# A decayed-attention scan: the output product and the bias in fp32r passes, softplus in two pieces, results in place, and part of the values' work on GpSimd

## The reference

```
q = x @ W_q.T;  k = x @ W_k.T;  v = x @ W_v.T          # 64 positions, 8 heads of 64
b = (q * k).sum(-1) * SCALE                             # one number per head and position
a = -softplus(x @ W_alpha_w.T + W_alpha_b).sum(-1)      # one number per head and position
vs, vl = sign(v), log(|v| + EPS)
step: ln = logaddexp(a_t + ln, b_t)
      dec, new = a_t + nm, b_t + vl_t;  m = max(dec, new)
      ssum = sg * exp(dec - m) + vs_t * exp(new - m)
      sg = sign(ssum) (0 counts as +);  nm = m + log(|ssum| + EPS)
      y_t = (sg * exp(nm - ln)).sum over heads
out = y @ W_o.T
```

## Time and profile before

| | |
|---|---|
| median of 3 runs | 2053.11 us (2052.66 to 2054.73) |
| the profiled execution | 2054.83 us, span 2053.0 us |
| granted TensorE clock, mean | 0.941 of full |
| busy over the span | TensorE 1886.5, VectorE 1333.0, ScalarE 1125.2, GpSimd 136.0 us |
| decayed attention layer | about 1516 to 1831 us |

### The profile page before, as it was taken

One profiled execution on the slowest core, in us unless ns is written; L12 is line 12 of the kernel. 1 busy time (PEld: TensorE's weight loads), 2 busy tenths in 40 slices (PEclk: granted clock), 3 DMA queues, 4 the chain that ended last, 5 costly groups with the idle time before them and its releaser, 6 DMA issues. The chain is left out here.

```text
span 2053.0 us, 31444 instructions
## 1 busy us (share of the span) xinstructions
PE 1886.5 (92%) x10506; PEld 1503.4 (73%) x10506; DVE 1333.0 (65%) x2451; ACT 1125.2 (55%) x1864; POOL 136.0 (7%) x130
## 2 busy tenths in 40 slices
PE   7989985999997599999999999999968999889998
PEld 4657875999996578787878787878746767665664
DVE  4783547999995373636363636363538898877686
ACT  5762324888884353535454545454426676656663
POOL 0001000111110010000000000000000000002221
PEclk9999976999998799999999999999988988879999
DMA  6300042453524121101010101012031000020000
GB/s 234 107 31 1 2 167 82 162 195 125 193 72 174 62 83 42 36 31 39 27 50 17 51 15 51 15 51 81 17 119 63 1 1 1 1 88 0 1 21 21
DMA packets 22753, 129.81 MB, mean 63 GB/s; under 512 B 3602, under 2 KB 3858, under 8 KB 18963
## 3 DMA queue, kind: packets, MB, share of 16 engines
q1 hardware_dynamic: 17714, 112.59, 15.1%
q0 software_dynamic: 4960, 16.26, 2.4%
HBM read 116.51 MB, written 12.32 MB: 63 GB/s over the span
## 5 line engine op out<-in xcount | busy, mean ns | idle before, releaser
L116 PE MATMUL PS<-cT,qs 128*128 128x512 f32 x1152 | 300.3, 406 | 2.3 <-DVE qs L1682 2.2
L116 PE MATMUL PS<-pT,cN 128*128 128x512 f32 x1152 | 270.1, 392 | 1.7 <-DVE pT L1682 1.7
L116 PEld LDWEIGHTS PS<-cT,qs 128*128 128x128 f32 x1152 | 210.6, 189 | 52.3 <-issue 7.9
L116 PEld LDWEIGHTS PS<-pT,cN 128*128 128x128 f32 x1152 | 213.9, 188 | 45.4 <-DVE pT L1682 1.9
L116 PE MATMUL PS<-fw,xgT 128*128 128x384 f32 x1104 | 204.5, 340 | 5.7 <-DVE xgT L1224 5.7
L116 PEld LDWEIGHTS PS<-fw,xgT 128*128 128x128 f32 x1104 | 193.3, 190 | 9.2 <-DVE xgT L1224 6.3
L1677 DVE TENSOR_REDUCE nmax<-PS 128x1 f32<-128x512 f32 x128 | 87.6, 684 | 162.6 <-PE PS L116 162.5
L1224 DVE TENSOR_TENSOR fw<-W,fw 128x1536 fp32r<-128x1536 f32 x92 | 159.2, 1752 | 22.8 <-ACT fw L1147 22.8
L116 PE MATMUL PS<-xT,ws 128*128 128x512 f32 x576 | 155.1, 422 | 15.1 <-PEq L2575 8.7
L1582 ACT ACTIVATE qp<-PS 128x512 f32<-128x512 f32 x96 | 57.4, 598 | 189.6 <-PE PS L116 189.6
L1147 ACT ACTIVATE fw<-W 128x1536 fp32r x92 | 134.4, 1489 | 33.1 <-issue 33.1
(11 more groups left out here) (285 smaller groups left out, 3398.9 us busy)
## 6 DMA issues: line engine op xcount, KB each, us to landing
W<-in_fc SPq DMA_DIRECT2D x8, 3072.0 KB, 11.1
cT<-in_ctxT SPq DMA_DIRECT2D x16, 768.0 KB, 4.3
raw_pj<-in_proj SPq DMA_DIRECT2D x8, 1536.0 KB, 6.5
ct_in<-in_ctxT SPq DMA_DIRECT2D x16, 768.0 KB, 4.3
cn_in<-in_ctxN SPq DMA_DIRECT2D x16, 768.0 KB, 5.0
W<-in_w SPq DMA_DIRECT2D x2, 4096.0 KB, 13.7
routed_y<-y POOLq DMA_DIRECT2D x23, 256.0 KB, 2.3
W<-in_w SPq DMA_DIRECT2D x5, 1024.0 KB, 7.3
```

The source lines that it names most:

```text
L116: mm = nc.tensor.matmul(out, lhs(m, s), rhs(n, s), start=(opens and (s, m, n) == terms[0]), stop=((s, m, n) == terms[-1]))
```

## The change

- Work areas: `lg`, `q`, `vt`, `v0`, `s_`, `ep` lie in W0 where six others lay. `mag`, `soft`, `qk`, `veps`, `ear` and `sg` are gone: softplus works in `lg`, the products in `q`, the signed epsilon is written to `vt` itself, and `ear`, the maximum and the signed result share `ep`. `bv`, `ebv`, `bal`, `y_raw` lie in W0 too.
- The bias product of the A projection is two fp32r products (`one` x two parts of `bal`).
- The output product is a `split_product` with `yT` and `wo` in two parts. ScalarE makes the first parts (`first_y`, and `wo` once at chunk 0, j=5), GpSimd the rests (`rest_y`, and `wo` in one 128x2048 instruction).
- `take_a` keeps Abs and Exp at j=1; `take_log` follows `take_q` at j=2. VectorE's `softplus` moves from j=2 to j=3, before the maximum, and `products` from before to behind the maximum of j=3.
- `make_v` on VectorE keeps only the bit operation; GpSimd adds (`vt = v0 + vt`), and GpSimd takes `rest_v`.
- w16's load also waits for the rest of `wo`, because `wo` is now loaded where w16 goes.

```
-            nc.tensor.matmul(bank, ones[0:1, :], bal[0:1, :], start=True, stop=False)
+            for part in range(2):
+                nc.tensor.matmul(bank, one[0:1, :], bals[part][0:1, :], start=(part == 0), stop=False)
...
-                    pe.wait_ge(yT_sb, BASE + 2 + c + 1)
+                    pe.wait_ge(y_lo, BASE + c + 1)
...
-                    for k in range(DK):
-                        mm = nc.tensor.matmul(ps[3], yT[:, c % 2, k, :], wo[:, k, :], start=(k == 0), stop=(k == DK - 1))
-                    mm.then_inc(z_mm, 1)
+                    split_product(nc, ps[3], lambda part, k: yT[part][:, k, :],
+                                  lambda part, k: wo[part][:, k, :], DK).then_inc(z_mm, 1)
...
 GpSimd
+                def make_v(c):
+                    pool.wait_ge(veps_sb, BASE + c + 1)
+                    nc.gpsimd.tensor_tensor(vt, v0, vt, ALU.add).then_inc(vt_sb, 1)
+                def rest_v(c):
+                    pool.wait_ge(v_hi, BASE + c + 1)
+                    nc.gpsimd.tensor_tensor(vs[1][:, c % 2, :], vt, vs[0][:, c % 2, :].bitcast(F32),
+                                            ALU.subtract).then_inc(v_lo, 1)
+                def rest_y(c):
+                    pool.wait_ge(y_hi, BASE + c + 1)
+                    pool.wait_ge(z_mm, BASE + c)
+                    nc.gpsimd.tensor_tensor(yT[1][:, :, :].rearrange("p k t -> p (k t)"), y_raw,
+                                            yT[0][:, :, :].rearrange("p k t -> p (k t)").bitcast(F32),
+                                            ALU.subtract).then_inc(y_lo, 1)
+                ln.pool(pool, 0)
+                ln.pool(pool, 1)
+                make_v(0)
+                rest_v(0)
                 for c in range(NG):
-                    ln.pool(pool, c)
+                    if c + 2 < NG:
+                        ln.pool(pool, c + 2)
+                    if c + 1 < NG:
+                        make_v(c + 1)
+                        rest_v(c + 1)
+                    if c == 0:
+                        pool.wait_ge(wo_hi, BASE + 1)
+                        nc.gpsimd.tensor_tensor(wo[1][:, :, :], wo_in, wo[0][:, :, :].bitcast(F32),
+                                                ALU.subtract).then_inc(wo_lo, 1)
+                    else:
+                        rest_y(c - 1)
...
+                rest_y(NG - 1)
...
 ScalarE
-                    nc.scalar.activation(mag, mag, ACT.Exp, scale=-1.0).then_inc(ex_sb, 1)
+                    nc.scalar.activation(lg, lg, ACT.Exp, scale=-1.0).then_inc(ex_sb, 1)
+                def take_log(c):
                     act.wait_ge(ex_sb, BASE + c + 1)
-                    act.wait_ge(a_used, BASE + c)
-                    nc.scalar.activation(lg, mag, ACT.Ln, bias=cn[:, CN_ONE:CN_ONE + 1]).then_inc(lg_sb, 1)
+                    nc.scalar.activation(lg, lg, ACT.Ln, bias=cn[:, CN_ONE:CN_ONE + 1]).then_inc(lg_sb, 1)
...
+                def first_y(c):
+                    act.wait_ge(yT_sb, BASE + 2 + c + 1)
+                    act.wait_ge(z_mm, BASE + c)
+                    nc.scalar.activation(yT[0][:, :, :].rearrange("p k t -> p (k t)"), y_raw, ACT.Copy).then_inc(y_hi, 1)
...
                 first_w(0)
+                act.wait_ge(s_bal, BASE + 16)
+                nc.scalar.activation(one[:, :], ones[0:1, :], ACT.Copy)
+                nc.scalar.activation(bals[0][:, :], bal, ACT.Copy).then_inc(bal_hi, 1)
                 first_w(1)
...
                         elif j == 2 and c + 1 < NG:
                             take_q(c + 1)
-                        elif j == 3 and c + 1 < NG:
-                            first_v(c + 1)
+                            take_log(c + 1)
+                        elif j == 3:
+                            if c + 1 < NG:
+                                first_v(c + 1)
+                            if c >= 1:
+                                first_y(c - 1)
+                        elif j == 5 and c == 0:
+                            act.wait_ge(s_wo, BASE + 16)
+                            nc.scalar.activation(wo[0][:, :, :], wo_in, ACT.Copy).then_inc(wo_hi, 1)
...
                 take_y(NG - 1)
+                first_y(NG - 1)
...
 VectorE
                     nc.vector.tensor_scalar(veps[:, :].bitcast(U32), v0[:, :].bitcast(U32), SIGN_BIT, EPS_BITS,
-                    nc.vector.tensor_tensor(vt, v0[:, :], veps[:, :], ALU.add).then_inc(vt_sb, 1)
-                def rest_v(c):
...
                 rest_w(0)
+                ve.wait_ge(bal_hi, BASE + 1)
+                nc.vector.tensor_tensor(bals[1][:, :], bal, bals[0][:, :].bitcast(F32), ALU.subtract).then_inc(bal_lo, 1)
                 rest_w(1)
...
                         elif j == 3 and c + 1 < NG:
-                            products(c + 1)
-                        elif j == 4 and c + 1 < NG:
-                            rest_v(c + 1)
+                            softplus(c + 1)
...
-                            nc.vector.tensor_tensor(ep[:, cols], ear[:, cols], ebv[:, t % 2, cols],
+                            nc.vector.tensor_tensor(ep[:, cols], ep[:, cols], ebv[:, t % 2, cols],
...
-                        elif j == 2 and c + 1 < NG:
-                            softplus(c + 1)
+                        elif j == 3 and c + 1 < NG:
+                            products(c + 1)
...
 SP
-                sp.dma_start(wo[:, :, :], a["w5"][:, W5_O]).then_inc(s_wo, 16)
+                sp.wait_ge(w_lo, BASE + 1)
+                sp.dma_start(wo_in, a["w5"][:, W5_O]).then_inc(s_wo, 16)
                 sp.wait_ge(w_lo, BASE + 4)
+                sp.wait_ge(wo_lo, BASE + 1)
                 sp.dma_start(e.w16, a["w16"]).then_inc(e.s_w6, 16)
```

More of the change, by code:

```diff
@@ L1794, in decayed_attention_layer @@
         ws = [sbuf(f"ws5{part}", [P, 4, DK, D], F32R) for part in range(2)]
-        mag, lg, soft, q, qk, vt = (W0[:, 8192 + n * D:8192 + (n + 1) * D] for n in range(6))
+        lg, q, vt, v0, s_, ep = (W0[:, 8192 + n * D:8192 + (n + 1) * D] for n in range(6))
         pick_in = W0[:, 11264:11264 + G * P]
-        wo = W0[:, 12288:12288 + DK * D].rearrange("p (k n) -> p k n", k=DK)
+        y_raw = W0[:, 11264:11264 + D]
+        bv, ebv = (W0[:, 12288 + n * 2 * D:12288 + (n + 1) * 2 * D].rearrange("p (n d) -> p n d", n=2) for n in range(2))
+        bal = W0[0:1, 14336 - D:14336]
+        wo_in = W0[:, 0:DK * D].rearrange("p (k n) -> p k n", k=DK)
+        wo = [sbuf(f"wo5{part}", [P, DK, D], F32R) for part in range(2)]
         rb = W0[:, 14336:14336 + RB * D].rearrange("p (n d) -> p n d", n=RB)
@@ L1802, in decayed_attention_layer @@
         vs = [sbuf(f"vs5{part}", [P, 2, D], F32R) for part in range(2)]
-        bal = sbuf("bal5", [1, D])
+        bals = [sbuf(f"bals5{part}", [1, D], F32R) for part in range(2)]
+        one = sbuf("one5", [1, P], F32R)
         xT = [[sbuf(f"xT5{u}{part}", [P, DK, P], F32R) for part in range(2)] for u in range(2)]
-        v0, veps = sbuf("v05", [P, D]), sbuf("veps5", [P, D])
         ba, spread, own = sbuf("ba5", [P, 2 * HS]), sbuf("spread5", [P, G, 2 * HS]), sbuf("own5", [P, 2 * G, HS])
@@ L1810, in decayed_attention_layer @@
                                                                        "eal5", "ebe5"))
-        bv, ebv = sbuf("bv5", [P, 2, D]), sbuf("ebv5", [P, 2, D])
-        ear, s_, ep, sg = (sbuf(n, [P, D]) for n in ("ear5", "s5", "ep5", "sg5"))
-        yT = sbuf("yT5", [P, 2, DK, P])
+        yT = [sbuf(f"yT5{part}", [P, DK, P], F32R) for part in range(2)]
         ln = Norm(nc, e, "5", sbuf, ps[3], xT[0])
         s_x5 = [sem(f"s_x5_{c}") for c in range(NG)]
+        bal_hi, bal_lo, wo_hi, wo_lo = sem("bal_hi5"), sem("bal_lo5"), sem("wo_hi5"), sem("wo_lo5")
+        y_hi, y_lo = sem("y_hi5"), sem("y_lo5")
         s_wk, s_wo, s_bal, s_pick = sem("s_wk5"), sem("s_wo5"), sem("s_bal5"), sem("s_pick5")
@@ L1839, in _ @@
                 sp.dma_start(w_in[:, 3], a["w5"][:, W5_K]).then_inc(s_wk, 16)
[L1840 removed]
+                sp.dma_start(bal, a["ba5"]).then_inc(s_bal, 16)
                 sp.wait_ge(e.s_xd, BASE + 16 * NT)
@@ L1930, in _ @@
                 pe.sem_inc(y_mm, RB)
-                pe.wait_ge(s_bal, BASE + 16)
+                pe.wait_ge(bal_lo, BASE + 1)
                 turn_x(0)
@@ L1980, in take_v @@
                     act.wait_ge(vt_sb, BASE + c)
-                    nc.scalar.activation(v0[:, :], ps[0], ACT.Copy).then_inc(v_sb, 1)
+                    nc.scalar.activation(v0, ps[0], ACT.Copy).then_inc(v_sb, 1)
                 def first_v(c):
@@ L2008, in take_y @@
                     act.wait_ge(y_mm, BASE + RB + G * (c + 1))
-                    act.wait_ge(z_mm, BASE + max(c - 1, 0))
-                    nc.scalar.activation(yT[:, c % 2].rearrange("p k (b j) -> p k j b", b=B),
+                    act.wait_ge(y_lo, BASE + c)
+                    nc.scalar.activation(y_raw.rearrange("p (k b j) -> p k j b", b=B, k=DK),
                                          ps[6 + c % 2].rearrange("p (k j b) -> p k j b", k=DK, j=G),
```

(10 more changed lines are left out.)

25 lines of the change are left out of this document (10 added, 15 removed).

## The result

Against the kernel before at 2053.11 us, the changed kernel takes **2058.15 us** (median of 15 runs): a ratio of 1.0023, 95% interval 1.0015 to 1.0031. It is slower by 5.0 us, where 12.0 were forecast; the sign and the size of a GpSimd hold came out and the time lies in the forecast range, but the length of the scan did not come out. Its profiled execution has a span of 2056.4 us, 3.4 more than before.

The account below looks back on a forecast made before the run. The prediction took VectorE to bound the scan's chunks. Its terms, -8.4 - 5.1 + 16.2 + 5.0 + 5.5 - 1.2, sum to +12.0 us, giving 2065.1 us against the median of 2053.11; range 2052 to 2079.

Parts of the forecast that it names:

- (a): VectorE in the scan loop: seven `vt` adds and seven `vs` subtractions removed, 0.60 us each, -8.4 us.
- (b): Softplus in two pieces in the scan: shorter waits before `ep` and for K, new wait for the logarithm, -5.1 us.
- (c): GpSimd takes adds and rests in the scan; its operations hold VectorE, about 2 us fall into waits, +16.2 us.
- second rival: VectorE's waits in the scan swallow half the GpSimd holds: +3.9 us, 2057 us; chance 0.17.
- (d): Rest of `wo`, one GpSimd instruction in steps 6 and 7 of chunk 0, holds VectorE: +5.0 us, once.
- (e): Tail: the last rest of `y` queues behind the rs6 power, so the last output product starts later, +5.5 us.
- (f): Last chunk's `add_out` wait goes and the prologue's bias product shortens, its split hidden by a 1.20 us wait: -1.2 us.
- third rival: TensorE drops to its slow clock more often, A projection late in all seven chunks: +6.4, 2072 us; chance 0.15.
- the first: Rival: GpSimd and VectorE operations of 256 columns slip past each other without holds: -9.2, 2044 us; chance 0.10.

Follow-up runs that it names:

- run 1: Kernel before with only the logarithm moved behind the copy of q, softplus to step 3 and products behind it: 2051.39 us, 0.9996.
- run 15: Kernel before with the logarithm split off the softplus and TensorE's head sums issued one step late: 2048.1 us, 0.9972.
- run 2: Changed kernel with the logarithm back behind Exp at step 1, softplus at step 2, products before the maximum of step 3: 2062.39 us, 1.0049.
- runs 5 and 6: Kernel before plus seven GpSimd adds of a tile nobody else reads, holding `s` of step 5 (first) or step 2 (second): 1.0005 and 1.0001.
- run 3: Changed kernel with the `vt` add back on VectorE: 2059.14 us, 1.0031.
- run 4: Changed kernel with the output product in plain fp32, without rests of `y` or `wo`: 2044.98 us, 0.9963.
- run 9: Kernel before plus seven GpSimd adds of a tile nobody else reads, holding the first operation of step 4: 1.0026, +3.8 to +5.3 us.
- run 13: Changed kernel with the last chunk's rest of `y` issued ahead of the power on GpSimd: 2054.34 us, 1.0011.
- run 14: Kernel before with the bias product alone in fp32r passes, split behind the second weight block: 2047.34 us, 0.9966.
- run 7: Changed kernel with the bias loaded ahead of K's weights and its split moved behind the second weight's: 2055.84 us, 1.0013.
- run 11: Kernel before with TensorE's head sums issued one step late, behind the next step's value product: 2046.86 us, 0.9972.
- run 10: Kernel before with three quarters of each of the first seven output products left out, result not the layer's: 2054.38 us, 1.0011.

## Why the prediction was right and where it failed

(a) Right. The fourteen instructions that are gone had 9.6 us of VectorE's busy time by their groups (seven of 692 ns, seven of 681), for 8.4 forecast, which took off the overlap.

(b) Right in its first half: the waits before `ep` shrink. The net worth was wrong: -5.1 was forecast, and alone run 1 gives -1.3, which can't be told from nothing, and run 15 nothing. In the change it is worth 4.2, by another way that the prediction missed: it puts the rest of `vs` beside `products` (run 2).

(c) The size of a hold was right: 1.05 for each add and about 1.1 for each rest of `y`. The rests of `vs`, with the 0.5 chosen between 0 and 1.05, cost 0.15 each, as `spread` shows. The holds come to 21.1 us with `wo`, or 19.9 by the busy time (10.3 more with 9.6 gone), for 23.2 forecast. **The step that failed is the one after it: that each hold counts on the path but for 2 us.** It rested on reading VectorE as the bound of the whole chunk, and its argument against the second rival (the adds sit ahead of the `ear` on which ScalarE's chain starts) was wrong: runs 5 and 6 show holds in steps 5 and 2 swallowed whole, run 3 shows it for the add, and run 4 fits with it for half of the `y` rests. Only in step 4 was a hold seen to count (run 9: +3.8 to +5.3 us for 5.5 of hold). If the logarithm's order took no waits away, as in runs 1 and 15, holds stood in for some 7.5 us of waits, where 2 were forecast.

(d) Right in size: 4.3 for 5.0. That it counts in full is argued, from its being longer than any wait before `ep` (3.92); no run takes it out alone.

(e) Right, 5.2 for 5.5, and run 13 shows its cause: with the rest ahead of the power 3.7 of them go.

(f) **The term that was mis-sized: the bias.** 0.4 us were given to it, on the prologue's path, and none in the loop; alone it gives 5.8 (run 14). The prediction saw the late A projections and their price, but took them as given, and its third rival had them getting more frequent. Three of seven projections ran at the low clock; with the shorter bias alone these three ran at the high one, and only the scan's first took 4.61. No run puts the fp32 bias back into the changed kernel, but there too all seven take 3.07. The other half of (f) failed too: the split of the bias was not covered by the 1.20 us wait, since ScalarE stood 3.07 us for the bias's transfer with weights queued behind it:

```profile
1521.79 0.31 ACT L2061 ACTIVATE one<-cn 1x128 fp32r<-1x128 f32 x1 [3.07 <-DMA W<-in_ba]
```

The first statistics came 2.3 us later after the layer's entry, of which 0.6 was left at the first `s`; with the split moved (run 7) the first `s` comes 2.6 us sooner.

The sum of the scan, then: 6.9 forecast, -3.0 measured, a miss of 9.9. Of this the bias makes 5.8 (run 14), the smaller busy time 4.5 (+10.3 for +14.8). The remaining idle time fell by 7.5 (13.3 less the bias's 5.8) for 7.9 forecast, a near match that is luck: the forecast put 5.1 of it on the logarithm and 2 on holds, and runs 1, 3, 5, 6 and 15 put it on holds that stood in for waits. So in the sum these two errors cancel, and what is left of the miss is the bias and the busy time. The parts aren't strictly additive, and no run separates them all. What the runs do measure are two sums: the fp32r output product costs 12.3 to 13.2 us (run 4), and everything else in the change saves 7.6 to 8.1 (2044.98 us, ratio 0.9963).

Of the rivals, the first is refuted (halves are held), the third too (no A projection in the changed kernel's scan ran at the low clock). The second, at 2057 us with a chance of 0.17, was nearest: it named a mechanism that the runs show. It swallows more than they do (8.1 us besides the 2, for some 7.5 in all), and it lacks the bias.

What stays open: why TensorE's clock fell on those three projections and not on the others. The engine was busy in the microseconds before and during each of them. Run 11 has the same fp32 bias and no slow one, run 14 a shorter bias and one (the first, at 1555.1, and there TensorE had waited 1.03 us shortly before), run 10 less work and one (at 1728.8). So both the work ahead of the projection and its order bear on it; no run says how.

## What to carry to other kernels

Before pricing a hold or a saving on the busiest engine, ask at each step who waits for that step's result: the same 0.8 us per chunk cost nothing in two steps and most or all of it in a third. A short instruction ahead of a long one that others wait for deserves a price of its own; here 0.4 us less of bias a chunk was worth 5.8 in all, by way of the clock of the product behind it. And a pass that needs an operand split pays for the split: the fp32r output product was off the path where it got faster, and its rests were on it (+12.3 to +13.2); without it the rest of the change is faster than the kernel before, 0.9954 with the bias split later.

## What the runs showed of the hardware

A GpSimd operation beside two-operand instructions of VectorE that follow without a gap may hold one at once or late. Six of seven adds of 1.3 us are recorded as 2.42, the first 1.15 beside `sg` and `new` halves at full speed, and hold only the next step's `s`; the seventh (1.39) holds the `sg` beside it, and the rest of `wo` holds the `new` that starts 0.16 us behind it. The prediction's reading, that GpSimd gets in between such instructions, fits the last two; what decides it stays open. A GpSimd add whose two inputs are one and the same tile takes 1.144 us, for 1.28 of the rests, and holds VectorE 0.8:

```profile
L1867 POOL TENSOR_TENSOR twice<-twice 128x512 f32<-128x512 f32 x7 | 8.0, 1144 | 150.0 <-DVE W L2233 150.0
```

And TensorE was granted its low clock in the midst of unbroken work: the same 12 passes took 4.61 us at a granted 0.62 in the kernel before and 3.07 at 1.00 in run 14, and both lengths stand in one and the same scan.
